# A flamingo block on one core: the last stage's beginning tile by tile, with another head and growth order

## The reference

```python
x = x + tanh(g_xattn[0]) * L0_xattn(layernorm(x), ctx)    # 16 heads; 16x16 scores within each row
x = x + tanh(g_ffn[0])   * L0_ffn(layernorm(x))           # shared GEGLU + the one expert with the largest logit of 8
x = x + tanh(g_xattn[1]) * L1_xattn(ctx, ctx, layernorm(x))  # one head of 256, softmax over the sample's 512 rows
x = x + tanh(g_ffn[1])   * L1_ffn(layernorm(x))           # 256 -> 1024, butterfly (10 stages), gelu, butterfly, -> 256
```

## Time and profile before

| | |
|---|---|
| median of 3 runs | 742.47 us (741.07 to 743.64) |
| the profiled execution | 742.7 us, span 740.9 us, mean granted TensorE clock 0.979 |
| busy share of the span | PE 93%, PEld 80%, DVE 84%, POOL 58%, ACT 55% |
| chain that ended last | PE 64%, DVE 12%, POOL 8%, issue 6%, ACT 5%, DMA 3% |
| 92 to 240 us | PE busy 147.6 of 148 us, DVE 145.6, POOL 142.1 |

### The profile page before, as it was taken

One profiled execution on the slowest core, in us unless ns is written; L12 is line 12 of the kernel. 1 busy time (PEld: TensorE's weight loads), 2 busy tenths in 40 slices (PEclk: granted clock), 3 DMA queues, 4 the chain that ended last, 5 costly groups with the idle time before them and its releaser, 6 DMA issues.

```text
span 740.9 us, 12939 instructions
## 1 busy us (share of the span) xinstructions
PE 688.1 (93%) x4381; PEld 590.0 (80%) x4381; DVE 619.9 (84%) x911; ACT 411.1 (55%) x760; POOL 426.9 (58%) x304
## 2 busy tenths in 40 slices
PE   5739999999999899999999999999967899999998
PEld 4518888888888888577778888888856899989988
DVE  3888999999999846699999999999877867687654
ACT  2324554545545411457867778887533575456653
POOL 3898999999999950413999776669031301220000
PEclk9969999999999999999999999999989999999999
DMA  9501100011155211424155516010010101000000
GB/s 279 224 6 34 49 29 28 28 47 38 29 174 227 69 29 44 133 90 183 36 199 199 199 42 237 29 29 16 17 35 15 51 22 58 30 29 8 8 15 29
DMA packets 28642, 56.43 MB, mean 76 GB/s; under 512 B 3408, under 2 KB 24656, under 8 KB 27440
## 3 DMA queue, kind: packets, MB, share of 16 engines
q1 hardware_dynamic: 23408, 47.64, 18.2%
q0 software_dynamic: 1872, 5.11, 2.5%
q10 hardware_dynamic: 3312, 3.02, 1.2%
HBM read 48.55 MB, written 7.21 MB: 75 GB/s over the span
## 4 chain that ended last, share of the span: by engine, by line
PE 64%; DVE 12%; POOL 8%; issue 6%; ACT 5%; DMA 3%; SPq 1%; DVEq 0%; ACTq 0%; POOLq 0%
PE bank L742 29%; PE bank L751 20%; PE bank L1004 8%; PE bank L759 4%; POOL PRODV L624 4%; POOL PRODV L626 2%; DVE SLOT_r L2004 2%; DVE PRODV_r L2004 2%; DVE STC L2092 1%; ACT L1516 1%; DMA XS<-normal_rows,INV 1%; DMA COLS<-cols 1%; DVE bank L1625 1%; ACT XS L1516 1%; DVE NM L2142 1%
## 5 line engine op out<-in xcount | busy, mean ns | idle before, releaser
L624 POOL TENSOR_TENSOR PRODV<-SHARED 128x2048 f32<-128x2048 f32 x32 | 144.5, 4516 | 10.5 <-DVE bank L1697 5.6
L742 PE MATMUL bank<-ROWS,SLOT 128*128 128x128 f32 x1024 | 122.1, 278 | 0.4
L742 PEld LDWEIGHTS bank<-ROWS,SLOT 128*128 128x128 f32 x1024 | 117.5, 193 | 2.9 <-ACT G L1241 2.8
L718 POOL TENSOR_TENSOR RS<-VE,MHALF 128x2 f32<-128x2 f32 x16 | 13.1, 818 | 151.5 <-DVE VE L2099 151.5
L1616 DVE TENSOR_TENSOR PRODQ<-bank,SHARED 128x4096 f32<-128x4096 f32 x16 | 70.8, 4423 | 6.9 <-PE bank L742 6.1
L626 POOL TENSOR_TENSOR PRODV<-PRODV 128x1024 f32<-128x1024 f32 x32 | 74.8, 2339 | 2.5
L1625 DVE TENSOR_REDUCE bank<-PRODQ 128x256 f32<-128x4096 f32 x16 | 70.7, 4419 | 0.1
L641 POOL DMA_INDIRECT XS<-normal_rows,INV x23 | 29.0, 1260 | 65.1 <-PE bank L759 43.3
L2004 DVE TENSOR_TENSOR PRODQ_r<-SLOT,ROWS_r 128x1024 fp32r<-128x1024 f32 x44 | 62.2, 1445 | 0.0
L742 PE MATMUL bank<-SLOT,HA 128*128 128x256 f32 x256 | 60.1, 389 | 1.8 <-DVE HA L1811 1.8
L742 PEld LDWEIGHTS bank<-SLOT,HA 128*128 128x128 f32 x256 | 48.5, 194 | 15.6 <-DVE HA L1811 9.2
(11 more groups left out here) (286 smaller groups left out, 1919.7 us busy)
## 6 DMA issues: line engine op xcount, KB each, us to landing
SLOT<-wexp SPq DMA_DIRECT2D x9, 3072.0 KB, 11.9
ROWS<-xT SPq DMA_DIRECT2D x16, 128.0 KB, 2.2
SHARED<-ctxT SPq DMA_DIRECT2D x16, 128.0 KB, 2.3
X<-x SPq DMA_DIRECT2D x16, 128.0 KB, 2.5
normal_rows<-ROWS SPq DMA_DIRECT2D x16, 128.0 KB, 1.7
WET<-ctxT SPq DMA_DIRECT2D x4, 512.0 KB, 8.2
out<-X SPq DMA_DIRECT2D x16, 128.0 KB, 1.7
expert_rows<-YS ACTq DMA_DIRECT2D x12, 128.0 KB, 1.7
```

The lines of the kernel that those rows point to most:

```text
L624: gp.tensor_tensor(o, pr, v, ALU.mult).then_inc(s["av_prod"], 1)
L742: last = pe.matmul(dst, lhs(k), rhs(k), start=(k == 0), stop=(k == chunks - 1))
```

## The change

- **Loads.** CTX of tile 0 and WKV0 come before XT; X of tile 0 comes in two halves; WO0, WG and GATE come after tile 2's loads.
- **Head.** TensorE makes the keys of tile 0 (into PB[6]) before queries(0) and the values after; ScalarE copies each by itself; `scores(0)` waits for q and the keys alone. VectorE does guarded_first(0) after scores(0). For tiles 1 to 3 queries follow keys and values at once. `grown_up` comes before first_root(0). The tanh of the gates moves behind `fold_up`.
- **Growth order.** PLACE and TOPS move to PRODQ behind the coefficients, and the down coefficients are grown in KV[:, 0] and EC right after GpSimd's last weighted values, with second_root(T-1) before the last product.
- **Last stage.** Unit 0: each tile has its own semaphores' counts, for gather, rows, root, normalised rows, flips (tile 0 in PB[5], tile 1 in PB[0]), copy and split; the two halves of fold(1) lie between and behind the flips; queries(0) takes two banks, one for each half of the width, each copied and split by itself. Unit 1's rows and statistics move into `first_unit`, behind largest(0).

`after(u, name)` gives the counts that follow from one more signal in unit 0 (u + 2 in place of u + 1); the other lines that only change counts are left out below.

```diff
...
-            load_turned(0, 0)
+            sp.dma_start(CTX[:, 0, :, :], ctxT[:, 0:P].rearrange("(k p) t -> p k t", p=P)).then_inc(w_in, 16)
             sp.dma_start(WKV0[:, :, :], wkv0.rearrange("(k p) n -> p k n", p=P)).then_inc(w_in, 16)
-            sp.dma_start(X[:, 0, :], x[0:P, :]).then_inc(tile_in[0], 16)
+            sp.dma_start(XT[0], xT[:, 0:P].rearrange("(k p) t -> p k t", p=P)).then_inc(tile_in[0], 16)
+            for h in range(2):
+                rows = slice(h * P // 2, (h + 1) * P // 2)
+                sp.dma_start(X[rows, 0, :], x[rows, :]).then_inc(tile_in[0], 16)
             load_tile(0, 1)
...
                 if (t0 := of(0)) is not None and first(t0, 1):
+                    grown_up()
                     first_root(t0)
-                    grown_up()
...
             sweep_a(gp, step)
-            second_root(T - 1)
+            gp.wait_ge(coef_in[1], 16)
+            v = COEF[1][:, 0:16]
+            for k in reversed(range(LOW - 1)):
+                if k == 0:
+                    second_root(T - 1)
+                w = (KV[:, 0, :] if k % 2 else EC)[:, 0:1024 >> k]
+                grow_down(k, v, w)
+                v = w
...
                     product(PB[5][:, 0:D], lambda k: rounded(ONES[:, :]), lambda k: WQ0[:, k, :], KD,
-                            s["wq_mean"])
+                            s["early_ps"])
+                    pe.wait_ge(w_in, 32)
+                    product(PB[6][:, 0:D], lambda k: CTX[:, 0, k, :], lambda k: WKV0[:, k, 0:D], KD, s["early_ps"])
                     pe.wait_ge(s["wq_ready"], 1)
                     queries(t0)
-                    pe.wait_ge(w_in, 16)
-                if t0 is not None:
+                    product(PB[4][:, D:2 * D], lambda k: CTX[:, 0, k, :], lambda k: WKV0[:, k, D:2 * D], KD,
+                            s["kv_done"])
+                elif t0 is not None:
...
                     product(PB[4][:, :], lambda k: CTX[:, t0[1], k, :], lambda k: WKV0[:, k, :], KD,
                             s["kv_done"])
-                    if first(t0, 2) and not first(t0, 1):
+                    if t4 is None:
+                        queries(t0)
+                    if first(t0, 2):
                         pair_products()
...
+                fill(("queries", 0), lambda bank, full: make(bank, full, [0]))
+                fill(("queries", 0, 1), lambda bank, full: make(bank, full, [1]))
...
-            flips(PB[0], 0, 0, "c_xn", "c_xT")
-            fold(1)
+            def fold_between_flips(bank, full):
+                for q, flipped in enumerate((PB[5], PB[0])):
+                    pe.wait_ge(c["c_xn"], q + 1)
+                    for k in range(KD):
+                        last = pe.transpose(flipped[:, (KD * q + k) * P:(KD * q + k + 1) * P],
+                                            XNC[:, q, k * P:(k + 1) * P], IDENT[:, :])
+                    last.then_inc(c["c_xT"], 1)
+                    product(bank[:, q * D:(q + 1) * D], lambda k: EC[:, (2 + q) * P:(3 + q) * P],
+                            lambda k: Z[:, 2 + q, :], 1, full if q else None)
+            fill(("fold", 1), fold_between_flips)
             queries(0)
...
                 largest(0)
+                next_rows(1)
+                next_stats(1)
                 lower_fold(3)
                 norm_rows(1, 0, "c_rstd", "c_xT", "c_xn")
                 shares(0)
...
+            def first_rows(q):
+
+                if q:
+                    dve.wait_ge(gathered[0], 16)
+                else:
+                    dve.wait_ge(first_in, 16)
+                dve.scalar_tensor_tensor(X[:, q, :], YG[:, q, :], TG[:, 2:3], X[:, q, :], ALU.mult, ALU.add)\
+                    .then_inc(x2_added, 1)
+                dve.wait_ge(x2_added, q + 1)
+                norm_stats(q, q, q, "c_stats", "c_agg")
+                dve.wait_ge(c["c_agg"], q + 1)
+                dve.tensor_scalar(VE[:, q:q + 1], MVC[:, q:q + 1, 1], EPS, None, ALU.add).then_inc(c["c_eps"], 1)
...
             lower_fold(0)
-            next_rows(0)
-            next_stats(0)
+            first_rows(0)
             lower_values(1, 0)
-            norm_rows(0, 0, "c_rstd", "c_xT", "c_xn")
+            first_rows(1)
+            first_normal(0)
             lower_values(1, 1)
-            lower_rows(PB[0], 0, "c_xT_hi", XN3T, XN3TL, "c_xT_sb")
+            first_normal(1)
+            first_lower(0, PB[5])
+            first_lower(1, PB[0])
             lower_fold(1)
-            next_rows(1)
-            next_stats(1)
             lower_queries(0)
             lower_fold(2)
             first_unit()
```

More of the change, by code:

```diff
@@ L469, in _ @@
             load_tile(1, 0)
+            for w, src in ((WO0, wo0), (WG, wg)):
+                sp.dma_start(w[:, :, :], src.rearrange("(k p) n -> p k n", p=P)).then_inc(wg_in, 16)
+            sp.dma_start(GATE[:, :], gates.partition_broadcast(P)).then_inc(wg_in, 16)
             sp.dma_start(WET[:, :, :], weT.rearrange("(c p) d -> p c d", p=P)).then_inc(we_in, 16)
@@ L723, in _ @@
             gather(1)
-            roots(0, 0, "c_eps", "c_rstd")
+            for q in range(2):
+                gp.wait_ge(c["c_eps"], q + 1)
+                gp.tensor_tensor(RS[:, q:q + 1], VE[:, q:q + 1], MHALF[:, :], ALU.pow).then_inc(c["c_rstd"], 1)
             roots(1, 0, "c_eps", "c_rstd")
@@ L847, in step @@
                     normal_rows(t3)
-                if t0 is not None and not first(t0, 1):
+                if t0 is not None and t4 is not None:
                     queries(t0)
@@ L1107, in scores @@
                 if n % 2 == 0:
-                    _, k, before = ring("queries", n // 2)
-                    pe.wait_ge(ring_free[k], before + 1)
+                    for use in [("queries", n // 2)] + [("queries", 0, 1)] * (n == 0):
+                        _, k, before = ring(*use)
+                        pe.wait_ge(ring_free[k], before + 1)
                 if n:
@@ L1487, in copies @@
             def copies(bank, u, turned, dst, signal):
-                act.wait_ge(c[turned], u + 1)
+                act.wait_ge(c[turned], after(u, turned))
                 act.activation(f32r(pair(dst)), by_row_tile(bank), ACT.Copy).then_inc(c[signal], 1)
             def queries(u):
-                bank, k, before = ring("queries", u)
-                act.wait_ge(ring_full[k], before + 1)
                 for m in range(KD):
+                    bank, k, before = ring("queries", u) if u or m == 0 else ring("queries", 0, 1)
+                    if u == 0 or m == 0:
+                        act.wait_ge(ring_full[k], before + 1)
                     act.activation(f32r(QT[:, m, :]), bank[:, m * U:(m + 1) * U], ACT.Identity,
@@ L1590, in _ @@
                 values(1, r)
-            copies(PB[0], 0, "c_xT", XN3T, "c_xT_hi")
+            for q, flipped in enumerate((PB[5], PB[0])):
+                act.wait_ge(c["c_xT"], q + 1)
+                act.activation(f32r(pair(XN3T)[:, q]), by_row_tile(flipped)[:, q], ACT.Copy).then_inc(c["c_xT_hi"], 1)
             fold(1)
@@ L1723, in step @@
                     scores(t1)
+                    if first(t1, 1):
+                        guarded_first(t1)
                 if t4 is not None:
@@ L1736, in step @@
                     row_max(t1)
-                if t0 is not None:
+                if t0 is not None and not first(t0, 1):
                     guarded_first(t0)
@@ L2070, in lower_queries @@
             def lower_queries(u):
[L2072 to L2073 removed]
                 for m in range(KD):
+                    bank, k, _ = ring("queries", u) if u or m == 0 else ring("queries", 0, 1)
+                    dve.wait_ge(c["q_high"], KD * u + (m + 1 if u == 0 else KD))
                     last = dve.scalar_tensor_tensor(f32r(QTL[:, m, :]), bank[:, m * U:(m + 1) * U], BK[:, m:m + 1],
                                                     rounded(QT[:, m, :]), ALU.add, ALU.subtract)
[L2077 removed]
+                    if u == 0 or m == KD - 1:
+                        last.then_inc(ring_free[k], 1)
             def lower_rows(bank, u, high, dst, lo, signal):
[L2081 removed]
+                dve.wait_ge(c[high], after(u, high))
                 lower(pair(lo), by_row_tile(bank), pair(dst), c[signal])
```

103 lines of the change are left out of this document (53 added, 50 removed).

## The result

The changed kernel takes 734.37 us (median of 5, 733.40 to 735.47) against 741.33 (740.86 to 743.64) for the kernel before: ratio 0.9899, 95% interval 0.9879 to 0.9919. In three later measurements of the same two kernels the ratio was 0.9939, 0.9944 and 0.9914, so this first one shows more than the others. The profiled execution is the median one, 734.37 us, span 732.6 instead of 740.9.

What follows compares the result with a forecast made beforehand. Bounds by stretch: the COLS load and GpSimd first, TensorE from 92 to 240 us, TensorE alternating with VectorE, then unit 0's gathers. 1.7 + 0.5 + 0.2 + 2.0 = 4.4 us gave 738.1 us against the median; range 735.1 to 741.2.

Steps and rivals of the forecast that it cites:

- step 4: Between the flip of tile 0's normalised rows and the gate: queries(3) gone, GpSimd's restart earlier; 0.5 us, bounds 0 and 1.1.
- The growth order: End of the first stage: moved growth costs nothing, fetch(2) leaves earlier and TensorE waits less; 0.2 of 0 to 0.35 us.
- port rule: VectorE and GpSimd take common SBUF ports in turn; growth might slow the first stage's drain by some 0.5 us, left out.
- The head: Start to GpSimd's first products: COLS lands 0.95 us earlier, a filled pause may keep TensorE's clock up; 1.7 us, ends 0.75 and 2.6.
- The last stage: Unit 0's start: scores 2.2 us earlier at half clock, 3.3 at full, 0.7 given back; 2.0 us taken.
- The clock stays up at both places: Rival: full clock at the pair products and unit 0's flips, tile 1's gather landing sooner; 735.1 us, chance 0.16.
- Queries in front, slower: Rival: at the start, late WKV0 or X makes queries(1) delay the pair products by 2.2 us; 743.7 us, chance 0.06.
- In vain: Rival: gather landings still limit the last stage, at most 0.2 there, and the start gives only 0.75; 741.5 us, chance 0.18.

Runs made afterwards that it cites:

- slot experiment: The kernel before with the head's edits, and slot 2's 3 MB load waiting for the third flip instead of the second: 738.54 us, 0.9948.
- spread statistics: The changed kernel with the statistics bunched between the largest of unit 0 and of unit 1 spread into VectorE's idle stretches: 737.09 us, 0.9931.
- its control: The changed kernel, unaltered, measured once more as the pair of the one with idle matmuls: 734.76 us, 0.9914.

## Why the prediction was wrong

The forecast was 4.4 us and the first measurement 7.0. In its pair of traces the spans differ by 8.3 us: 4.2 by GpSimd's first start (forecast 2.2, step 4 included), 1.0 from there to the last stage's gather (forecast 0.2), 3.1 behind it (forecast 2.0). By the four measurements together it is 5.8 us, and two of the four (0.9939, 0.9944) lie beside the 4.4 (0.9941). That is luck: the experiments make the growth order's term far too small, and the head's and the last stage's, by the medians, as large as I had them or smaller.

**The growth order (0.2): the step that failed.** I took the wait of one trace, 0.35 us, for all that could be won, and 0.2 of it, as "VectorE ... sets the next step"; the low end of the range had no more than the 0.35. In that trace fetch(2) had left 0.7 us before the 3 MB. I wrote that it would now go out "before the 3 MB of slot 2", and priced that at nothing. In the five other traces with the old order and the old slot wait the 3 MB went first, by 1.4 us, and the third flip came 11.1 to 12.1 us behind the second where the growth order has 7.9. Three of the five are without the head's edits. What they share, and the first trace has not, is down_rows at 3.70 us instead of 5.39: TensorE's full clock brings the flips forward against the fetches, while a lead of the head moves both alike. From GpSimd's first start to the last stage's gather the six traces with the old order take 513.8 to 517.4 us (mean 515.8), the thirteen with the growth order 512.6 to 514.0 (mean 513.4). So the order is worth 2.4 us in the mean, and by the ratios 2.0 to 3.2, not 0.2. With 2.4 in its place the forecast would have been 6.6 us and the low end of the range near 733. The slot experiment shows the cause. What stays open is why the head alone gave so little: five of its twelve runs are below every run of before beside them (740.02 and up), and the only trace is of a slower one.

The moved growth itself cost nothing, as forecast. The operations of VectorE beside it, which read or write PSUM on one side, took as long as before (0.42, 0.47 and 0.68 us); the pair with both operands in SBUF does not stand there, so the port rule that I had weighed against it was not put to the test.

**The head (1.7; was 4.2 in the result's trace).** The mechanism stood: scores at 9.53 instead of my 10.5, no gain by itself; the end hung on COLS and the clock. Both sizes were off. I valued COLS at 0.95 us by issue time and bytes. Over the traces that is about right for the mean (17.3 without the head's edits, 16.4 in nine of twelve with them), but in the other three the loads landed by 15.0, and then 2.5 us come. The clock I took as the middle between 0 and 1.7. It isn't a middle: without the head's edits the pair products took 5.05 to 6.4 us in all five traces that had no idle work added, with them 3.46 to 3.56 in eight of twelve (the run with the three loads put back and the one with idle work left out). So the likelier value was the rival's. By GpSimd's first start the head is worth 2.4 us in the mean of these traces (24.0 to 24.9 without, 20.1 to 24.6 with), 4.2 in the result's. The times show less: 0.9988 alone, and 1.0 us on top of the other two parts.

**Step 4 (0.5; was 0).** With queries(3) gone from there the product of half the hidden row (32 matmuls) began 2.0 us after the flip and not 2.9; but that much earlier more of it fell into the half clock, and it took 5.27 us instead of 4.32. The restart came no further forward than the start.

**The last stage (2.0; was 3.0 to 4.0 in the traces).** Given back: 0.78 (predicted 0.7, and shown by the spread statistics). The start: in the result's trace tile 1's rows came 6.40 us after the first gather's issue, nearly as before (6.63); from there to the scores it took 6.85 us instead of 10.63, where I had 8.4 with the half clock and 6.55 with the full one. The clock was the full one in all four traces of the changed kernel; I took it for the half one. That is most of the term. Where the old order had the full clock too (the slot experiment), gather to scores took 14.16 us and gather to end 199.6, against 199.0 to 199.7 for the changed kernel and 202.6 to 203.0 for five others of the old order. So at equal clock the new order gives some 0 to 0.7 us. The full clock was there in eight of twelve traces with the new order and in one of six with the old (those with idle work left out); the run with queries(1) late has the changed kernel's last stage and had 0.72 there. Medians give less than traces: head and growth with it against without, 0.9939 to 0.9947; head alone 0.9982 to 0.9988, each difference within the intervals. The term's size in the median stays open, somewhere between 0 and 4.0 us.

**The rivals.** "The clock stays up at both places" is what the first trace shows (735.1 forecast, 734.37 measured), less the 0.6 for an earlier landing of tile 1's gather, and with COLS' early landing in its place. That gather took 5.0 us there (5.2 before); in two of the other three traces of the changed kernel the rows came 5.8 us after the first gather's issue instead of 6.4 to 6.5, and gather to end was 0.6 to 0.8 us shorter, as the rival had it. Its chance of 0.16 was too small: I had its price right and had no row for what a shorter pause does. "Queries in front, slower" did not occur: WKV0 landed 5.0 us after its issue, in time for the key product at 7.37. "In vain" is out: all four measurements are faster than its 741.5.

## What to carry to other kernels

Where two queues issue transfers whose order depends on a race of about a microsecond, price both orders: here a small gather behind a 3 MB load took three times its landing, and one trace showed only one of the two orders. When an edit shows little alone, compare its trace with that of before stage by stage, and ask of every stage whether a second trace of before has the same. Test the wait that releases the large transfer first, as it is one number. A clock or landing that varies makes a term two-valued: take the likelier value and a chance, not the middle, and trace the same kernel more than once.

## What the runs showed of the hardware

An indirect fetch from GpSimd's queue landed in 3.1 to 3.4 us alone, and in 9.1 to 10.1 when issued 1.4 us behind SyncE's 3 MB, though they stand in different queues (software and hardware dynamic in the profile). Issued 0.7 us ahead of the 3 MB, in the first trace of before, it still took 8.6; 4.3 us ahead, in the changed kernel, 3.4. The Trainium skill (DMA: Bandwidth & Descriptors, Queues, rings and completion order) has each DMA engine alternate between queues packet by packet. By that rule a small fetch shares with the large load and does not stand behind it; the trace cannot show the turns, but the threefold landing shows that sharing is no protection here.

COLS' 6 KB took 3.6 and 3.7 us when issued ahead of the megabyte of coefficients and the four weights, and 6.3 to 8.5 behind them, but the group's last landing did not clearly move (by 15.0 and at 16.1, against 14.7 to 16.8 in the changed kernel): the waiter waits for the last load of the group, whichever it is.

TensorE's granted clock fell at other places from one execution to the next of the same kernel: 1.00, 0.70 or 0.54 over the pair products of the changed one. With idle matmuls before them they ran at 1.00 in both kernels tried; in the changed one the idle matmuls outlasted the pause, the pair products began at 18.32 us, and the kernel was 3.6 us slower than its control by the medians.
